# Moving VectorE's x_lo and product parts behind its evacuations, and GpSimd's copy of the next x directly behind the weave

## What is computed

```python
x = x + conv(x, L0_weight, groups=4, taps=9) + bias of (cond, side)      # L0
x = x + mix(x, L1) ; x = x + mix(x, L2)                                  # L1, L2
x = x + conv(x, L3_weight, groups=4, taps=9) + bias of (cond, side)      # L3
# mix(x): att = softmax(gelu MLP of cond); W = sum_k att[k] * weight[k]; W @ x + att @ bias_k
```

## Time and profile before

| engine | busy us | share of the span | instructions |
|---|---|---|---|
| TensorE matmul | 606.3 | 97% | 12658 |
| TensorE weight load | 470.0 | 75% | 12658 |
| VectorE | 502.6 | 81% | 1006 |
| ScalarE | 402.6 | 65% | 750 |
| GpSimd | 276.3 | 44% | 170 |

### The profile page before, as it was taken

One profiled execution on the slowest core, in us unless ns is written; L12 is line 12 of the kernel. 1 busy time (PEld: TensorE's weight loads), 2 busy tenths in 40 slices (PEclk: granted clock), 3 DMA queues, 4 the chain that ended last, 5 costly groups with the idle time before them and its releaser, 6 DMA issues.

```text
span 622.9 us, 28330 instructions
## 1 busy us (share of the span) xinstructions
PE 606.3 (97%) x12658; PEld 470.0 (75%) x12658; DVE 502.6 (81%) x1006; ACT 402.6 (65%) x750; POOL 276.3 (44%) x170
## 2 busy tenths in 40 slices
PE   8998999999999999999999999999999999999985
PEld 6885788777778777777777777877778777777775
DVE  7898688888887787888787888778788878788655
ACT  5756566667667667667666766666766766676643
POOL 5134355345345435435634535543544553453240
PEclk9999999999999999999999999999999999999998
DMA  8156757667877666876666787776687666656616
GB/s 250 58 217 170 206 175 217 214 186 194 233 177 192 209 208 162 234 205 184 198 212 183 198 229 177 192 211 203 168 236 197 191 196 214 182 139 172 168 73 204
DMA packets 50703, 118.88 MB, mean 191 GB/s; under 512 B 5749, under 2 KB 26410, under 8 KB 42842
## 3 DMA queue, kind: packets, MB, share of 16 engines
q1 hardware_dynamic: 49170, 116.04, 66.9%
q0 software_dynamic: 704, 1.26, 0.6%
q10 hardware_dynamic: 776, 0.89, 0.5%
HBM read 35.33 MB, written 33.55 MB: 111 GB/s over the span
## 4 chain that ended last, share of the span: by engine, by line
PE 85%; DVE 8%; issue 3%; DMA 1%; ACT 1%; POOL 1%; SPq 1%; DVEq 0%
PE ps L1143 36%; PE ps L1156 31%; PE ps L1300 10%; PE ps L1132 4%; DVE out_taps L909 2%; DVE prod_sum L951 2%; DVE x_lo L875 1%; PE ps L1278 1%; PE ps L1252 1%; DMA out_sb<-in_L_cond_weight 1%; DMA out_planes<-out_taps 1%; DVE x_in L1013 1%; POOL out_sb L529 1%; SPq L421 0%; DVE x_full L1016 0%
## 5 line engine op out<-in xcount | busy, mean ns | idle before, releaser
L529 POOL COPY out_sb<-out_planes 128x2048 f32<-128x2048 f32 x30 | 121.7, 4057 | 169.1 <-issue 124.2
L512 POOL COPY x_full<-x_in 128x2048 f32<-128x2048 f32 x29 | 116.4, 4015 | 126.4 <-DVE x_lo L875 119.8
L1156 PE MATMUL ps<-z_full,taps_raw 32*32 32x512 f32 x2880 | 122.2, 596 | 0.9 <-issue 0.9
L899 DVE SCALAR_TENSOR_TENSOR z_lo<-ps,bias_tab,z_hi 128x1024 fp32r<-128x1024 f32 x62 | 76.8, 1280 | 36.3 <-ACT z_hi L694 36.3
L1156 PE MATMUL ps<-x_full,taps_raw 32*32 32x512 f32 x2880 | 102.2, 598 | 0.0
L702 ACT ACTIVATE out_taps<-ps,bias_tab 128x512 f32<-128x512 f32 x62 | 39.3, 686 | 88.4 <-PE ps L1143 85.8
L889 DVE SCALAR_TENSOR_TENSOR y_lo<-ps,bias_tab,y_hi 128x512 fp32r<-128x512 f32 x128 | 87.2, 744 | 10.6 <-ACT y_hi L684 10.6
L1156 PEld LDWEIGHTS ps<-z_full,taps_raw 32*32 32x32 f32 x2880 | 73.5, 103 | 25.8 <-issue 2.7
L1300 PE MATMUL ps<-y_hi,mix_w 32*128 32x512 f32 x1024 | 87.6, 385 | 0.1
L694 ACT ACTIVATE z_hi<-ps,bias_tab 128x1024 fp32r<-128x1024 f32 x62 | 65.8, 1113 | 29.4 <-PE ps L1300 29.4
L684 ACT ACTIVATE y_hi<-ps,bias_tab 128x512 fp32r<-128x512 f32 x128 | 77.0, 682 | 7.3 <-PE ps L1156 5.1
(11 more groups left out here) (174 smaller groups left out, 933.8 us busy)
## 6 DMA issues: line engine op xcount, KB each, us to landing
x_in<-in_x SPq DMA_DIRECT2D x31, 1024.0 KB, 7.4
out_planes<-out_taps SPq DMA_DIRECT2D x122, 256.0 KB, 4.7
out<-out_sb SPq DMA_DIRECT2D x30, 1024.0 KB, 4.5
mix_w<-prod SPq DMA_DIRECT2D x124, 128.0 KB, 3.8
x_in<-in_x SPq DMA_DIRECT2D x2, 512.0 KB, 5.2
out<-out_sb POOLq DMA_DIRECT2D x2, 512.0 KB, 3.5
out<-x_full SPq DMA_DIRECT2D x7, 128.0 KB, 3.0
out_taps<-in_L_cond_weight SPq DMA_DIRECT2D x1, 512.0 KB, 5.5
```

The source lines that it names most:

```text
L512: pool.tensor_copy(row_order(t, d, x[:, :, home(t, d)]), x_order(t, d, x_in[t.par(d)][:, :])).then_inc(x_planed, 1)
L529: pool.tensor_copy(x_order(t, d, out_sb[t.par(d)][:, :]), row_order(t, d, out_planes[:, :, :]))\
L899: dve.scalar_tensor_tensor(out=z_home(t, 0)[1][:, 2 * h:2 * h + 2, home(t, 0)], in0=ps[:, k:k + 2, :], scalar=bias_tab[:, b, 2 * G:BIAS], ...
L1156: tile = pe.matmul(ps[rows(p), first_bank + g, :], taps_raw[l][rows(g), d - p, :], full[rows(g), d % PH, c:c + S], start=(first and n == 0 ...
```

## The change

VectorE: `split_product` is cut in two. In a step, the reduction stays where it is; the parts of the product (L954, L956) and x_lo now come behind `evac_out`, ahead of z_lo, in all steps of `one`. ScalarE: the edges of x_lo come behind z_hi in all steps. GpSimd: `plane_x` no longer waits for x_lo and x_hi of the sample before; its waits for the load and for conv0 stay. Which instructions are issued is the same.

```diff
--- before.py
+++ after.py
@@ -505,8 +505,6 @@
             def plane_x(t, d):
                 b = t.i + d
                 pool.wait_ge(x_loaded[t.par(d)], DMA * (t.pair(d) + t.par(d)))
-                pool.wait_ge(x_lo_done, b)
-                pool.wait_ge(x_hi_done, b)
                 pool.wait_ge(conv0_done, G * (b - 1))
                 x = x_full[t.par(d)]
                 pool.tensor_copy(row_order(t, d, x[:, :, home(t, d)]), x_order(t, d, x_in[t.par(d)][:, :])).then_inc(x_planed, 1)
@@ -754,12 +752,9 @@
                     evac_out(t, -1)
                 else:
                     evac_out(t, -1)
-                    if t.at(1):
-                        high_z(t)
+                    high_z(t)
                     if not plain(t, 1):
                         edges_low_x(t, 1)
-                    if not t.at(1):
-                        high_z(t)
                     if not plain(t, 0):
                         edges_z(t)
 
@@ -937,7 +932,7 @@
                     dve.tensor_tensor(out=lo, in0=mat[:, :], in1=hi.bitcast(F32), op=ALU.subtract)\
                        .then_inc(mats_lo_done, 1)
 
-            def split_product(t, d):
+            def split_product(t, d, parts=True):
                 b = t.i + d
                 dve.wait_ge(prod_done, G * (b + 1))
                 if t.at(1 - d):
@@ -950,6 +945,11 @@
                 if not t.at(1 - d):
                     dve.tensor_reduce(out=prod_sum[:, :], in_=prod_at(t, d).rearrange("m r (h z) -> m z h r", z=C), axis=AX.XY,
                                       op=ALU.add).then_inc(prod_summed, 1)
+                if parts:
+                    product_parts(t, d)
+
+            def product_parts(t, d):
+                b = t.i + d
                 dve.wait_ge(prod_summed, b + 1)
                 dve.tensor_copy(prod[:, 0, :], prod_sum[:, :]).then_inc(prod_hi_done, 1)
                 dve.wait_ge(prod_hi_done, b + 1)
@@ -980,17 +980,15 @@
                 if t.has(0):
                     low_y(t)
                 if t.has(1):
-                    split_product(t, 1)
-                if t.has(1) and not t.at(2):
-                    low_x(t, 1)
+                    split_product(t, 1, parts=False)
                 if t.at(N - 1):
                     last_taps_low()
                     low_z(t)
                     evac_out(t, -1)
                 else:
                     evac_out(t, -1)
-                    if t.at(2):
-                        low_x(t, 1)
+                    product_parts(t, 1)
+                    low_x(t, 1)
                     low_z(t)
 
             def last_taps_low():

```

## The result

The changed kernel takes 645.63 us (median of 4 runs, 644.74 to 646.61); the kernel before, 623.77 us on the same chip. The ratio is 1.035 (95% interval 1.033 to 1.037). The forecast was 652 us. The profiled execution took 645.52 us.

What follows compares the result with a forecast made beforehand. TensorE was taken to set the pace, VectorE's order costing it 0.42 us a sample. Steady +17.7, opening +3.5 and +2, middle +1.9 and end +2.8, together +27.9 on 624.8, gave 652.7, or 652 us beside the median; range 614 to 672.

Steps and rivals of the forecast that it cites:

- the block: VectorE operations with two SBUF inputs stand still until GpSimd's copy ends; meeting the copy at its start costs 4 us.
- the ring: Copy, parts, mix_w, relay, weave, next copy each wait for the one before: 19.1 us a turn against 18.42.
- the gain: Evacuation moved ahead removes TensorE's 0.42 us wait at conv0; VectorE's list at 18.08 us leaves 0.34 us a sample.
- m: Start of the first mix matmul of a sample on TensorE, 324.15 in the steady stretch of the kernel before.
- Steady: 26 steady samples at 19.1 instead of 18.42 us: +17.7 us.
- Opening: Sample 3's copy starts amid the matrix operations, which stand for its 4 us: +3.5; entering the ring: +2.
- Middle: bias_last's four DMAs on GpSimd's queue come between weave and copy, so into the ring once: +1.9 us.
- End: The last weave, awaited by the last convolution through z, comes at m + 13.4: +2.8 us.
- No block: Rival: no block by GpSimd's copy, or one too short to matter; 617 us, chance 0.22.
- Slight meeting: Rival: relay lands early, mat_lo releases the weave, 18.1 to 18.7 us a sample; 623 to 640 us, chance 0.13.
- Dragging relay: Rival: relay on SyncE's queue drags as at 68.59, 20.8 us a sample; 697 us, chance 0.08.
- Nothing on the path: Rival: other waits keep conv0 where it is, within 0.3%; 624 us, chance 0.05.

Runs made afterwards that it cites:

- short copy: Changed kernel with GpSimd copying only 64 of 512 positions of each plane of the next x, from sample 3 on: 620.91 us, ratio 0.989.
- split copy: Changed kernel with relay ahead of mix_w, edge copies and copy's fourth plane behind x_lo, sample 3's copy awaiting x_lo, bias_last's DMAs behind copy: 614.08 us, ratio 0.981.
- the kernel with the relay first: Changed kernel with the four relay DMAs ahead of mix_w's in SyncE's queue: 629.46 us, ratio 1.004.
- GpSimd's part alone: Kernel before the change, with only GpSimd's waits for x_lo and x_hi taken out: 688.5 us, ratio 1.099.
- GpSimd's waits put back: Changed kernel with GpSimd's waits for x_lo and x_hi put back, the rest as changed: 669.03 us, ratio 1.067.

## Why the prediction was right, point by point

The changed kernel is slower, by the block and the ring that were forecast; the sizes of the terms were less good than the total, as the sum shows.

- **What bounds, and the gain.** TensorE was held at conv0 for 0.42 us a sample; I put VectorE's own list at 18.08 us. The short copy and the split copy run at 18.05, and in the split copy the weight loads ahead of the product still wait for y_lo, 6.1 us in 24 samples. That the total is right to 0.03 us is in part luck: in one of its samples (m = 390.18) y_lo ends at 405.13, m + 14.95 instead of 14.87, and the product begins at 405.18, 0.05 us behind it instead of 0.15. TensorE by itself needs 17.99, so the two bounds lie 0.06 us apart. It is the gain that the change was after: it was there, and the ring took more.
- **The block.** Read from blocks that made an operation 0.07 to 0.09 us longer, and taken to last as long as the copy. The changed kernel shows long ones. VectorE, GpSimd and TensorE in the opening, and GpSimd and VectorE in the middle:

```profile
41.94 4.11 DVE L923 SCALAR_TENSOR_TENSOR mat<-mix_w,att_tab,acc 128x128 f32<-128x128 f32 x1
...
49.61 1.39 DVE L904 TENSOR_SCALAR out_taps<-ps,bias_tab 128x512 f32<-128x512 f32 x2
...
41.82 4.08 POOL L510 COPY x_full<-x_in 128x2048 f32<-128x2048 f32 x1
...
51.15 1.22 PE L1141 MATMUL ps<-x_hi,taps_hi 32*128 32x512 f32 x16 [2.53 <-DVE out_taps L904]
...
312.00 2.11 POOL L603 DMA_DIRECT2D bias_last<-bias_tab  x4
...
314.11 4.04 POOL L510 COPY x_full<-x_in 128x2048 f32<-128x2048 f32 x1
...
315.29 2.95 DVE L954 CAST prod<-prod_sum 128x128 fp32r<-128x128 f32 x1
```

  A matrix operation of 0.35 us took 4.11, ending at 46.05 with the copy ended at 45.90. A cast of 0.23 us took 2.95 and ended 0.09 us behind the copy (318.15). Operations with a PSUM input kept their length under such copies: y_lo (2.73 us, 328.73 under the weave), the evacuation (1.41 us for two, 334.93 under the copy). In these rows the trace agrees with the lock that the Trainium skill describes ("SBUF — State Buffer", section "SBUF: two separate sides"), which is held for the whole instruction. The cast has one SBUF input and would by that section be held only in a two-port mode; that it is held is shown, its mode is not.
- **The ring.** I had 10.5 + 8.15 + 0.45 = 19.1 us. The rows after give: parts' end to weave 337.34 to 347.62 = 10.28; weave to the copy's end 328.91 to 336.79 = 7.88; copy's end to parts' end 0.55. Together 18.71. The terms mis-sized are the first two: the weave began 7.5 us behind the relay's start, as in the steady rows, with nothing left for the rounding up to 10.5, and the copy follows the weave after 3.82 us, not 4.1, though the weave is listed with 4.01 us. The kernel before never runs a weave and a copy back to back. TensorE's idle time at the product, put at 1.1 us, is 0.48 us by the matmul rows; the turn is 0.7 to 0.8 us above TensorE's own 17.99.
- **The sum.** Steady: 24 samples at 18.76 us on average, +8.2 against my +17.7 for 26; the last one, 19.7 us, adds 1.3 that I hadn't. Opening: the fifth mix is 4.1 us later than before (107.12 and 103.03 for its first group), I had 5.5. Middle: 20.97 against 18.42, +2.5, of which 2.3 over the ring's own turn, where I had 1.9. End: the last convolution starts 26.45 us behind the mix of sample 30, 22.98 before: +3.5, I had 2.8 (the last weave is at m + 14.1, not 13.4: the parts end 2.2 us behind m, not 2.9, but the weave comes 11.9 us behind them). With the 1.4 of the next point that makes some 21 us, and the span grew by 20.8. The total of 27.9 was 7 too high. The steady term alone was 9.5 too high and the opening 1.4, and the last steady sample, the middle, the end and the last convolution took 4 us more than I had; so the total is nearer than its main term.
- **What was not in the sum.** The last convolution itself is 1.4 us longer. Weave, TensorE and the window of the changed kernel, then the same window of the kernel before:

```profile
612.14 4.00 POOL L527 COPY out_sb<-out_planes 128x2048 f32<-128x2048 f32 x1 [14.08 <-DMA out_planes<-out_taps]
...
624.48 0.80 PE L1250 MATMUL ps<-x_hi,taps_hi 32*128 32x256 f32 x8 [5.68 <-DVE x_lo L894]
...
624.00:632.00 8.00, 7.52 (x164) 7.52 (x168) 2.09 (x4) 0.28 (x2) 0.00 (x0) 0.61 0.55 135
```

```profile
605.00:613.00 8.00, 7.95 (x212) 7.95 (x216) 3.14 (x6) 1.05 (x3) 0.00 (x0) 0.79 0.53 135
```

  TensorE waits 5.68 us for z (it was 1.81) and then runs at a granted 0.61 instead of 0.79.
- **Rivals.** "No block" is refuted by the 4.11 us row; what it forecast is what the short copy gives. "Slight meeting" has the weave released by mat_lo, as in the kernel with the relay first (18.47 us a turn, 629 us), not in this one. "Dragging relay" didn't occur in the steady samples: landing 5.0 us in the rows read. "Nothing on the path" fell with the 0.23 us at conv0.

## What to carry to other kernels

Before an operation is moved, lay out which engine owns what the two share: here VectorE's operations with two SBUF inputs, and its cast, stood still for as long as a GpSimd copy ran (up to 4.11 us for 0.35), and only operations that read PSUM were free cover for it. In a queue that works in order, ask of each moved producer what stands behind its consumer; the relay, 2.5 us later behind the mix than before (5.51 against 2.97 us), took the weave over from mat_lo, and its place alone is worth about 15 us here (644.26 and 629.46 us, on two chips). It only lengthened the ring; with the relay first the ring still turned, at 18.47 us, over mat_lo. This ring was opened at several places at once: relay, edges, the first copy, bias_last's DMAs and a quarter of the copy together turned +2.8% into -1.9% beside the same kernel before.

## What the runs showed that I had not expected

- A stop of TensorE can cost more than its length, and the length alone doesn't say when. With GpSimd's part alone, the stops of 2.58 to 2.85 us at conv0, in every second sample, left a granted clock of 0.50 to 0.60 for the next 3 us, where 0.50 is the lower level (1.2 GHz) throughout. With GpSimd's waits put back, the stops of 1.52 to 1.74 us ahead of the product, in every sample from the seventh on, left it at 1.00; an earlier one of 1.93 us left 0.76. But the stop of 2.53 us in the changed kernel's opening (51.15) left it at 1.00 too, and one of 1.81 us ahead of the last convolution of the kernel before left 0.79 over 8 us. What decides between them wasn't tried.
- Taking GpSimd's waits away alone gave not a slower steady pace but a beat of two samples, 18.5 and 22.6 us.
- VectorE finished 0.07 to 0.11 us (cast) or 0.14 to 0.15 us (two inputs, in the rows read) behind the copy that held it: the mark by which such a block is found in a profile that names no releaser for it. One cast with GpSimd's part alone was held longer than its copy: it began at 336.83, the copy at 337.21, and it took 4.48 us; GpSimd was issuing bias_last's DMAs just then. Whether these hold VectorE as well wasn't tried.
